# Rewriting the prologue of a fused long-convolution and routed-LoRA kernel on one core

## What is computed

```python
dtA = (-exp(log_A_real) + 1j * A_imag) * exp(log_dt)[:, None]
K = 2.0 * einsum('hn,hnl->hl', Cc * (exp(dtA) - 1.0) / A, exp(dtA[:, :, None] * arange(L))).real
y = (irfft(rfft(u * mask) * rfft(K))[..., :L] + u * mask * D[:, None]) * mask
logits = einsum('bsd,ed->bse', y, route_w); gate = one_hot(argmax(logits)) * max(logits)
h = einsum('bsd,erd->bser', y, A)
out = x + einsum('bser,eor->bso', gate[..., None] * h, Bw)
```

## Time and profile before

| | |
|---|---|
| time, median of 3 runs | 608.7 us (608.7, 608.7, 610.63) |
| the profiled execution | 609.9 us, its span 608.1 us |
| PE busy | 581.6 us, 96% of the span |
| DVE, ACT, POOL busy | 81%, 52%, 63% |
| DMA | 77.64 MB, mean 128 GB/s |
| chain that ended last | PE 92%, DVE 3%, ACT 2% |

### The profile page before, as it was taken

The page is one execution under the profiler, slowest core; times in us unless marked ns, Lnnn a source line. Parts: engine busy times, 40 slices in busy tenths (PEclk is TensorE's granted clock), DMA queues, the critical chain, the costliest instruction groups (busy, mean ns, idle before and its releaser), DMA issues.

```text
span 608.1 us, 13318 instructions
## 1 busy us (share of the span) xinstructions
PE 581.6 (96%) x3617; PEld 529.0 (87%) x3617; DVE 490.3 (81%) x1371; ACT 317.2 (52%) x1059; POOL 385.9 (63%) x520
## 2 busy tenths in 40 slices
...
DMA packets 37582, 77.64 MB, mean 128 GB/s; under 512 B 12476, under 2 KB 20862, under 8 KB 37510
## 3 DMA queue, kind: packets, MB, share of 16 engines
q1 hardware_dynamic: 28358, 43.76, 28.8%
...
## 4 chain that ended last, share of the span: by engine, by line
PE 92%; DVE 3%; ACT 2%; issue 1%; POOL 1%; DMA 0%; ACTq 0%; POOLq 0%
PE psYo L1060 20%; PE psZ L1080 19%; PE psO L1060 15%; PE psYe L1060 13%; PE psS L1060 11%; PE psO L1107 5%; PE psXe L1071 5%; PE psXo L1071 5%; PE psZ L1136 1%; DVE psS L918 0%; DVE ex L758 0%; DMA logs<-in_L_cond_log_dt_dram 0%; POOL both L465 0%; DVE ost L957 0%; ACT L577 0%
## 5 line engine op out<-in xcount | busy, mean ns | idle before, releaser
L504 POOL TENSOR_TENSOR Slo<-Sf,Shi 128x384 fp32r<-128x384 f32 x64 | 65.3, 1021 | 166.1 <-ACT Shi L651 166.1
L918 DVE SCALAR_TENSOR_TENSOR psS<-Sf,tab,psS 64x128 f32<-64x128 f32 x256 | 91.9, 359 | 48.1 <-ACT Sf L646 41.2
L1080 PE MATMUL psZ<-Wt,Y 128*128 128x136 f32 x1024 | 129.2, 279 | 0.0
L1080 PEld LDWEIGHTS psZ<-Wt,Y 128*128 128x128 f32 x1024 | 123.3, 190 | 0.1
L646 ACT ACTIVATE Sf<-psS 128x128 f32<-128x128 f32 x64 | 17.8, 277 | 200.3 <-PE psS L1060 200.3
L957 DVE TENSOR_TENSOR ost<-psO,xt 128x512 f32<-128x512 f32 x128 | 87.7, 690 | 1.2 <-PE psO L1060 1.1
L497 POOL TENSOR_TENSOR Xlo<-xeven,Xhi 128x512 fp32r<-128x512 f32 x64 | 82.9, 1295 | 0.0
L465 POOL TENSOR_TENSOR both<-coarse,fine 128x512 f32<-128x512 f32 x64 | 69.0, 1079 | 1.3 <-ACT fine L591 1.2
L941 DVE TENSOR_TENSOR wlo<-psZ,whi 128x128 fp32r<-128x128 f32 x64 | 18.7, 292 | 41.2 <-ACT whi L656 41.2
L1060 PE MATMUL psYo<-Xhi,Thi 128*128 128x512 f32 x128 | 51.2, 400 | 0.0
L1060 PE MATMUL psYo<-Xlo,Thi 128*128 128x512 f32 x128 | 51.1, 399 | 0.0
...
## 6 DMA issues: line engine op xcount, KB each, us to landing
...
kdram<-krow SPq DMA_DIRECT2D x64, 1.0 KB
...
```

What stands on the lines that cost most here:

```text
L504: pool.tensor_tensor(Slo[h.s2][:, :], Sf[h.s2][:, :], Shi[h.s2][:, :].bitcast(F32), ALU.subtract).then_inc(slo_done, 1)
L918: dve.scalar_tensor_tensor(psS[to, new], Sf[h.s2][fr, old], tab2[fr, BR, h.n:h.n + 1], psS[to, new], ALU.mult, ALU.add).then_inc(brought_d ...
L1080: last = pe.matmul(psZ[:, 0:NW], Y[:, j, c, :], Wt[:, 2 * c + j, :], start=(j == 0 and c == 0), stop=(j == 1 and c == NE - 1), skip_group_ ...
```

## The change

Maths and results stay. (1) T is cut before it is skewed: `k_raw` copies the taps, `k_split` makes the high and the low part in a `kcol` twice as wide, both are transposed and written (two small DMAs a head) and skewed into `T` (four buffers, 256 KB a head for 128 KB); PE reads `T` at once, `t_hi` and `t_lo` are gone. (2) Nothing is read backwards per head: positions in a block run the other way, for which `posn` is reversed, and A and the router weights are reversed once (`A_rev` on POOL, `route_rev` on ACT). (3) Decay rates are packed, transposed and made into magnitudes first. (4) The orders of the prologue on all engines are rewritten, and four calls of `keep_warm` put matmuls of the identity by itself on PE that nobody reads; `from_states(0)` goes ahead of `within(0)`; some of the work on heads 2 to 7 moves into step 1. The diff without declarations, its core:

```diff
-        sp.dma_start(bass.AP(kdram.tensor, h.s2 * (P + Q), [[G32, P // G32], [P, 2], [1, G32]]),
-                     krow[h.s2][0:P:G32, :, :]).then_inc(k_out[h.s2], 16)
+        for part in range(2):
+            sp.dma_start(bass.AP(kdram.tensor, (h.s2 * 2 + part) * (P + Q),
+                                 [[G32, P // G32], [P, 2], [1, G32]]),
+                         krow[h.s2][0:P:G32, part, :, :]).then_inc(k_out[h.s2], 16)
...
-        need(sp, thi_done, h.n - 1)
-        need(sp, tlo_done, h.n - 1)
-        need(sp, k_out[h.s2], h.half * 16 + 16)
-        sp.dma_start(Traw[h.s2][:, :],
-                     bass.AP(kdram.tensor, h.s2 * (P + Q), [[1, P], [1, Q]])
+        need(sp, y_mm, (h.n - 3) * 2)
+        need(sp, k_out[h.s2], h.half * 32 + 32)
+        sp.dma_start(T[h.s4][:, :, :].bitcast(F32),
+                     bass.AP(kdram.tensor, h.s2 * 2 * (P + Q), [[1, P], [P + Q, 2], [1, Q]])
...
-    pool.iota(posn[:, :], pattern=[[P, NB]], base=0, channel_multiplier=1,
...
+    pool.wait_ge(rho_tab, 1)
+    exponents(pool, *RHO_PARTS[0])
+    pool.wait_ge(in_A, 16)
+    pool.tensor_copy(A_rev[:, :, :],
+                     A_nat[:, :].rearrange("p (c l) -> p c l", l=P)[:, :, ::-1]).then_inc(rev_done, 1)
...
-        pool.tensor_tensor(Glo[h.s4][:, :], Grev[h.s2][:, ::-1], Ghi[h.s4][:, :].bitcast(F32),
+        pool.tensor_tensor(Glo[h.s4][:, :], Grev[h.s2][:, :], Ghi[h.s4][:, :].bitcast(F32),
...
             s_lo(head(0))
         if head(1).there:
             x_lo(head(1))
-        if head(3).there and is_head(head(0), 1):
+        if is_head(head(0), 1):
+            g_lo(head(1))
+            weigh(parts[1])
             g_table(head(3))
-        if head(1).there:
-            t_lo(head(1))
+            g_lo(head(2))
         if head(3).there:
             g_lo(head(3))
...
     first = [Head(n) for n in range(4)]
-    exponents(pool, *RHO_PARTS[0])
     angle_steps(parts[0])
-    x_lo(first[0])
     turn_parts(parts[0])
     pool.wait_ge(rden_set, 2)
     pool.tensor_tensor(CA[:, :, :], Craw[:, :, :], over(rden[:, :]), ALU.mult).then_inc(ca_set, 1)
     pool.wait_ge(mag_done, 2)
     weigh(parts[0])
     g_table(first[0])
+    x_lo(first[0])
     g_table(first[1])
     g_lo(first[0])
     g_table(first[2])
     angle_steps(parts[1])
-    t_lo(first[0])
-    g_lo(first[1])
     s_lo(first[0])
     x_lo(first[1])
+    g_lo(first[1])
+    g_table(first[3])
     turn_parts(parts[1])
-    g_table(first[3])
-    g_lo(first[2])
-    weigh(parts[1])
-    t_lo(first[1])
-    g_lo(first[3])
...
-    act.activation(warm[:, :], quarter[:, :], ACT.Sin)
+    act.activation(warm[:, :], quarter[:, :], ACT.Exp)
...
+    def k_raw(h):
+        need(act, b_mm, h.n + 1)
+        need(act, klo_done, (h.n - 1) * 2)
+        act.activation(kraw[h.s2][:, 0:1], psB[:, 0, P:P + 1], ACT.Copy).then_inc(kraw_done, 1)
+        act.activation(kraw[h.s2][:, 1:2], psB[:, 1, P:P + 1], ACT.Identity,
+                       bias=Dcol[:, h.n:h.n + 1]).then_inc(kraw_done, 1)
...
+    def k_split(h):
+        need(act, kraw_done, h.n * 2 + 2)
+        need(act, k_turned, h.n - 1)
+        act.activation(kcol[h.s2][:, 0, :, 0:1], kraw[h.s2][:, :].rearrange("p (j a) -> p j a", a=1),
+                       ACT.Copy).then_inc(khi_done, 1)
+        need(act, khi_done, h.n + 1)
+        for j in range(2):
+            act.activation(kcol[h.s2][:, 1, j, 0:1], kcol[h.s2][:, 0, j, 0:1].bitcast(F32), ACT.Identity,
+                           scale=-1.0, bias=kraw[h.s2][:, j:j + 1]).then_inc(klo_done, 1)
...
         if head(2).there:
+            k_raw(head(2))
             b_hi(head(2))
+            k_split(head(2))
...
-            t_hi(head(1))
...
+        if is_head(head(0), 1):
+            g_hi(head(1))
+            mirror(parts[1])
+            g_hi(head(2))
             g_hi(head(3))
...
     first = [Head(n) for n in range(4)]
     x_hi(first[0], 0)
+    act.wait_ge(rho_turned, 1)
+    act.activation(tab1[:, RHO, :], psS[:, 0:H], ACT.Copy).then_inc(rho_tab, 1)
     x_hi(first[0], 1)
-    x_even(first[0])
+    act.wait_ge(rho_done, 1)
+    magnitudes(slice(0, 2 * FIRST))
+    act.activation(warm[:, :], quarter[:, :], ACT.Sin)
     act.wait_ge(tabs_turned, 1)
-    act.activation(tab1[:, :, :], psY[0][:, 0:4 * H].rearrange("p (t h) -> p t h", h=H),
+    act.activation(tab1[:, 0:RHO, :], psY[0][:, 0:RHO * H].rearrange("p (t h) -> p t h", h=H),
                    ACT.Copy).then_inc(tab_done, 1)
+    turns(parts[0])
     act.wait_ge(phases_done, 1)
     act.activation(sine[:, :, :], phase[:, :, :], ACT.Sin, scale=TURN).then_inc(sines_done, 1)
     act.activation(sine_half[:, :, :], phase[:, :, :], ACT.Sin, scale=TURN / 2).then_inc(sines_done, 1)
-    turns(parts[0])
-    act.wait_ge(rho_done, 1)
-    magnitudes(slice(0, 2 * FIRST))
     sines(parts[0])
-    for dst, src in weights():
-        act.wait_ge(w_turned, 1)
-        act.activation(dst, src, ACT.Copy).then_inc(w_done, 1)
+    x_even(first[0])
     mirror(parts[0])
+    act.wait_ge(in_rw, 16)
+    act.activation(route_rev[:, :, :], route_nat[:, :].rearrange("p (c l) -> p c l", l=P)[:, :, ::-1],
+                   ACT.Copy).then_inc(rev_done, 1)
     act.wait_ge(tabs_turned, 2)
     act.activation(tab2[:, :, :], psX[0][:, 0:5 * H].rearrange("p (t h) -> p t h", h=H),
                    ACT.Copy).then_inc(tab_done, 1)
     act.wait_ge(tab_done, 2)
     m_matrix(first[0])
+    m_matrix(first[1])
+    act.wait_ge(in_D, 16)
+    k_raw(first[0])
+    k_split(first[0])
+    b_hi(first[0])
+    act.wait_ge(route_turned, 1)
+    act.activation(Wt[:, :, 0:E], psS[:, 0:NB * E].rearrange("p (c w) -> p c w", w=E),
+                   ACT.Copy).then_inc(w_done, 1)
     for j in range(2):
         act.wait_ge(b_turned, j + 1)
         act.activation(Bw_hi[:, j * 512:(j + 1) * 512], psY[j][:, :],
                        ACT.Copy).then_inc(bhi_set, 1)
-    act.wait_ge(in_D, 16)
-    b_hi(first[0])
     g_hi(first[0])
-    m_matrix(first[1])
     first_state(first[0])
     x_hi(first[1], 0)
     x_hi(first[1], 1)
+    x_even(first[1])
+    k_raw(first[1])
     b_hi(first[1])
-    t_hi(first[0])
     s_hi(first[0])
+    k_split(first[1])
+    m_matrix(first[2])
     g_hi(first[1])
-    x_even(first[1])
+    for dst, src in weights():
+        act.wait_ge(w_turned, 1)
+        act.activation(dst, src, ACT.Copy).then_inc(w_done, 1)
+    k_raw(first[2])
+    b_hi(first[2])
+    k_split(first[2])
     turns(parts[1])
-    m_matrix(first[2])
-    b_hi(first[2])
-    g_hi(first[2])
+    m_matrix(first[3])
     sines(parts[1])
-    m_matrix(first[3])
-    t_hi(first[1])
-    g_hi(first[3])
-    mirror(parts[1])
...
-    dve.tensor_copy(pack1[:, :, 1, :], pack1[:, :, 0, :]).then_inc(pack1_done, 1)
+    dve.wait_ge(v_set, count[0])
+    STT(pack1[:, VL, :, :], over(w1), -c3, over(err[:, :]), ALU.mult, ALU.add).then_inc(pack1_done, 1)
+    link(horner(p, r, TAYLOR[3]), 1)
...
+            b_lo(head(2))
             turn_k(head(2))
-            b_lo(head(2))
...
+    whole_turns(parts[0])
     dve.wait_ge(v_set, count[0])
     dve.wait_ge(sines_done, 2)
     link(TT(Lm1[:, 1, :], e1, sine[:, 0, :], ALU.mult), 1)
     link(STT(cm1[:, :, :], sine_half[:, :, :], -2.0, sine_half[:, :, :], ALU.mult, ALU.mult), 1)
-    link(TT(pack2[:, BR, 0, :], sine[:, 1, :], e256, ALU.mult), 1)
+    fractions(parts[0])
...
-    dve.wait_ge(tab_done, 1)
-    exponents(dve, *RHO_PARTS[1])
+    masks(0, 3)
+    turn_k(first[0])
+    b_lo(first[0])
+    dve.wait_ge(tab_done, 2)
     for j in range(2):
         dve.wait_ge(bhi_set, j + 1)
         TT(Bw_lo[:, j * 512:(j + 1) * 512], psY[j][:, :],
            Bw_hi[:, j * 512:(j + 1) * 512].bitcast(F32), ALU.subtract).then_inc(blo_set, 1)
-    turn_k(first[0])
-    b_lo(first[0])
-    masks(0, 4)
-    dve.wait_ge(tab_done, 2)
     carry(first[0])
     x_lo(first[1])
+    b_lo(first[1])
     turn_k(first[1])
-    b_lo(first[1])
-    masks(4, NB)
+    exponents(dve, *RHO_PARTS[1])
+    masks(3, NB)
     whole_turns(parts[1])
     dve.wait_ge(mask_done, NB)
+    b_lo(first[2])
     turn_k(first[2])
-    b_lo(first[2])
     cut(first[0], 0)
     cut(first[0], 1)
     fractions(parts[1])
...
     def project(h):
+        if is_head(h, 0):
+            pe.wait_ge(w_done, 3)
-            pe.wait_ge(w_done, 3)
+            pe.wait_ge(w_done, 1)
     def within(h, j):
-        need(pe, thi_done, h.n + 1)
-        need(pe, tlo_done, h.n + 1)
-        T = [(Thi[h.s2][:, j, :], Tlo[h.s2][:, j, :]) for j in range(2)]
+        need(pe, t_in[h.s2], h.half * 16 + 16)
+        K = [(T[h.s4][:, 0, j * P:(j + 1) * P], T[h.s4][:, 1, j * P:(j + 1) * P]) for j in (1, 0)]
+        need(pe, y_masked, h.n * 2 - 1 + j)
+        products = [(K[0], X[j])] + [(K[1], X[0])] * j
-            pe.wait_ge(blo_set, j + 1)
-        need(pe, y_masked, h.n * 2 - 1 + j)
-        three(psY[j][:, :], [(T[0], X[j])] + [(T[1], X[0])] * j, True, False)
+            three(psY[j][:, :], products, False, True).then_inc(y_mm, 1)
```

(54 more changed lines are left out.)

102 lines of the change are left out of this document (45 added, 57 removed).

## The result

The changed kernel takes 615.0 us (614.36 to 615.43), the kernel before, run beside it, 608.7; the ratio is 1.0094, 95% interval 1.0072 to 1.0116. It is slower, by 0.9%. Profiled execution against profiled execution it is 615.4 against 609.9, and the spans, 613.6 and 608.1, differ by the same 5.5 us. Median against median it is 6.3 us, because the profiled execution of before is one of its longer ones: 12 of the 21 executions timed in a later round have spans of 606.6 to 606.9. Three places hold the 5.5.

A forecast was written before the change was run, and what follows sets the result against it. PE, busy 96%, was taken to bound the steady steps, leaving gains only ahead of step 3. With 2.4 GHz by about 20 us, 609.9 - 3.2 = 606.7 us, after 2.2 given back in step 2; range 604.6 to 611.6.

The forecast's parts named there:

- rival 1: Prologue: the clock rises only in PE's third busy stretch, near 30.5 us; 610.3 us, no change; chance 0.23.
- POOL is free from 9.2 to 12.4, so any of these is hidden: Prologue tables: `A_rev` on POOL costs 0.8 to 2.6 us, taken as 1.5, and delays nothing.
- that rule on the masks: First waves: by DVE's shared port, three masks push G of head 0 by 0.8 us; kept as upper end.
- The early rise of the clock: Prologue: PE's two early gapless stretches bring 2.4 GHz by about 20 us; 606.7 us instead of 610.3.
- From step 3 on ... nothing: Steady steps: `k_split` adds 0.5 on ACT, `t_hi` takes 0.4 away, POOL loses 0.7; steps stay 8.86 us.
- rival 3: Steady steps: T's doubled traffic or `k_split` delays `wh` by 0.05 in each of 61 steps; +3, 609.7 us; chance 0.06.
- PE's wait for `Grev` in step 2: Step 1 to 2: the added chain takes 5.75 us, PE's own way 4.5, so PE waits 1.25.
- The given-back 2.2 us: Step 1 to 2: `turn_wh(1)` starts 11.1 us after `turn_wh(0)`, where before it took 8.9; 2.2 lost again.

The follow-up runs named there:

- e2: The changed kernel with the reversal of A (`A_rev`) on ACT behind its copy of table 1, not on POOL: 612.33 us, ratio to before 1.006.
- e9: e8 with six more fillers behind the B transposes and six between `inputs(0)` and `bring(0)` in place of two behind `w_done`: 607.92 us, ratio 0.9978.
- e8: The changed kernel with the edits of e2 and e3 together: 612.09 us, ratio 1.0044.
- e10: e9 with three tiles (`kraw`, `krow`, the fourth `T`) declared last, no instruction changed: 605.8 us, ratio 0.9941.
- e11: The kernel before with two unused spare tiles, 1088 bytes a partition ahead of `Bhi` and 2048 ahead of `Sf`: 610.88 us, ratio 1.0013.
- e1: The changed kernel without its four `keep_warm` calls: 614.3 us, ratio to before 1.0085.
- e12: The changed kernel with 12 more tiny matmuls on PE, ahead of its wait for table 1: 615.0 us, ratio 1.0086.
- e3: The changed kernel with `weigh(parts[1])` in POOL's prologue, `g_hi` and `mirror` ahead of `w_hi(0)` on ACT, turns of heads 8 to 11 behind: 611.95 us.

## Why the prediction was wrong

Forecast 606.7, measured 615.0, above the range as well. The sum closes like this: rival 1 (late rise, 610.3), which is the case that came, + 1.3 for what step 3 starts later than that rival has it (1.73 for 0.4) + 1.55 for addresses + 2.2 for the end = 615.35, and the profiled execution has 615.43.

- **"POOL is free from 9.2 to 12.4, so any of these is hidden"** failed. The size was near (1.04 us in the range 0.8 to 2.6) and POOL did have the room, but I asked only whether POOL waits, not who works beside it. DVE's operation paid 0.87; `wave` came 1.24 late, and with it `inputs(0)` (23.72 for 22.15) and the taps of head 2 (38.32 for 36.8). e2 shows the cause of most of it: there `wave` starts at 16.74 and `inputs(0)` at 22.38. The other 0.39 of `wave` is no matter of `A_rev`, and no run was made for it. The Trainium skill, "Advanced Engine Details and Errata", section "VectorE Performance Modes" (Mode Summary), says that DVE's second SBUF port is shared with GpSimd, and that GpSimd's instructions and those of DVE that use both ports block each other. The 1.15 for 0.28 agrees, though the trace does not say which ports the operation used; I had put that rule on the masks only. There it cost POOL nothing: the first mask starts at 21.51, when `both` of head 0 has ended, and beside the three masks `Grev` took 0.72 and the next `both` 1.05, as without them. The masks paid, 1.0 each.
- **The early rise of the clock** failed. PE worked without a gap from 12.45 to 17.3 and through 20.5 to 24.6, and the first fast rows are at 31.90. That was rival 1's case, at 31.9 for its 30.5. The forecast put an early rise at 3.6 us (606.7 for 610.3). e9 against e8 shows 2.05 with the second half of the prologue at the high clock, and e8 had part of it already; the whole 3.6 no run shows.
- **"From step 3 on ... nothing"** failed by its premise, that a step of PE's own work cannot change when no instruction of it does. I set rival 3 at 0.05 a step through T or `k_split`; the size was half that and the mechanism another, the addresses of tiles (e10, e11).
- **The end of the kernel** had no term in the sum. It is a fetch of PE's instructions beside the last stores, 2.2 us. The four calls of `keep_warm`, which the sum took to cost nothing where PE waits anyway, bring most of it: without them it is 0.5 (e1), and with the list made longer still, 0.2 (e12).
- **What held.** `first_state(1)` 4.92 after the taps' copy (4.9 predicted), `turn_wh(0)` 4.44 after that (4.4), PE's wait for `Grev` in step 2 1.21 (1.25), `turn_wh(1)` 10.76 after `turn_wh(0)` (11.1), `both` to `wave` 2.68 (2.7), `both` itself 1.12 (1.1). The timeline rows of ACT behind the first two, in after:

```profile
38.32 0.17 ACT L611 ACTIVATE kraw<-psO 128x1 f32<-128x1 f32 x1 [2.61 <-PE psO L1124]
...
43.24 0.26 ACT L652 ACTIVATE Sf<-psS 128x128 f32<-128x128 f32 x1
```

The given-back 2.2 us was right in place and nearly in size: `turn_wh(1)` lags 1.86 more than before (10.76 for 8.90), and e3 returns 1.59 by its order of step 1.

The change can be made to pay: with `A_rev` moved, the order of step 1 as in e3, the fillers in the real gaps and three declarations at another place, the same work takes 605.8 us, 0.6% below the kernel before. What each of its own ideas gives by itself, T cut before it is skewed and the early magnitudes above all, was not measured.
